# A graph layer on one core: attention's steps laid out by TensorE's load, and seven in place of five pairs of edge tiles fetched by ScalarE's queue

## The reference

```
msg   = relu(x[src] + edge_attr @ w_e + b_e)              # 131072 edges
agg   = segment_sum(msg, dst)                             # src, dst sorted by dst
local = bn1(relu((x + agg) @ w1 + b1) @ w2 + b2 + x)
q,k,v = split(x.reshape(256, 32, 256) @ in_w.T + in_b)    # 256 graphs of 32 nodes
o     = softmax(q k^T / 8) v                              # 4 heads of 64
attn  = bn2(o @ out_w.T + out_b + x)
out   = local + attn
out   = bn3(out + relu(out @ m_w1 + m_b1) @ m_w2 + m_b2)
y     = layernorm(x + out)
```

## Time and profile before

| | |
|---|---|
| median of 3 runs | 1318.26 us (1317.13 to 1326.54) |
| the profiled execution | 1322.04 us, its span 1320.3 us |
| TensorE busy | 1164.2 us, 88% |
| GpSimd busy | 944.2 us, 72% |
| VectorE busy | 824.7 us, 62% |
| ScalarE busy | 543.6 us, 41% |
| mean granted clock of TensorE | 0.96 |

### The profile page before, as it was taken

The page is one execution under the profiler, slowest core; times in us unless marked ns, Lnnn a source line. Parts: engine busy times, 40 slices in busy tenths (PEclk is TensorE's granted clock), DMA queues, the critical chain, the costliest instruction groups (busy, mean ns, idle before and its releaser), DMA issues.

```text
span 1320.3 us, 28247 instructions
## 1 busy us (share of the span) xinstructions
PE 1164.2 (88%) x7309; PEld 650.1 (49%) x7309; DVE 824.7 (62%) x2090; ACT 543.6 (41%) x1077; POOL 944.2 (72%) x1004
## 2 busy tenths in 40 slices
PE   5777899899898989988898999989899898999787
PEld 3444454444444444444444445445454455666466
DVE  4665575848557465775747667584765857555464
ACT  1334344444343444533444443444444344344344
POOL 7466647777777777777677777777777777777771
PEclk6989999999989989999999999999999999999899
DMA  8354445565655556555465556556565555555551
GB/s 318 104 165 129 140 124 153 164 190 163 189 158 154 177 154 181 162 174 167 140 186 167 180 157 187 162 155 188 163 181 161 174 160 172 164 166 173 156 147 54
DMA packets 119282, 216.50 MB, mean 164 GB/s; under 512 B 24784, under 2 KB 69584, under 8 KB 119120
## 3 DMA queue, kind: packets, MB, share of 16 engines
q0 software_dynamic: 47808, 130.61, 34.3%
q1 hardware_dynamic: 67312, 79.47, 19.2%
q10 hardware_dynamic: 4000, 4.61, 1.0%
HBM read 197.82 MB, written 16.78 MB: 163 GB/s over the span
## 4 chain that ended last, share of the span: by engine, by line
PE 49%; DVE 14%; POOL 9%; issue 9%; ACTq 9%; ACT 7%; DMA 3%; DVEq 1%; SPq 0%; POOLq 0%
PE bank L839 27%; PE bank L869 11%; POOL xg L432 9%; PE bank L884 7%; ACTq L465 6%; ACT msg L471 4%; DVE bank L683 4%; ACTq L313 2%; DVE mx L728 2%; PE bank L893 2%; DVE dif L733 2%; PE bank L966 2%; DMA xg<-in_x_dram,srcs 2%; DVE aggT L716 2%; DMA xT<-in_xT_dram 1%
## 5 line engine op out<-in xcount | busy, mean ns | idle before, releaser
L432 POOL DMA_INDIRECT xg<-in_x_dram,srcs x996 | 943.3, 947 | 349.7 <-issue 285.3
L471 ACT ACTIVATE msg<-bank 128x512 f32<-128x512 f32 x512 | 277.9, 594 | 528.9 <-PE bank L869 280.8
L683 DVE TENSOR_TENSOR bank<-xg,bank 128x512 f32<-128x512 f32 x498 | 326.1, 689 | 184.2 <-ACT msg L471 97.2
L869 PE MATMUL bank<-we,ea 64*128 64x256 f32 x2048 | 303.2, 416 | 43.1 <-DVE bank L683 42.7
L869 PEld LDWEIGHTS bank<-we,ea 64*128 64x128 f32 x2048 | 185.1, 193 | 188.3 <-issue 145.0
L716 DVE TENSOR_TENSOR aggT<-bank,aggT 128x64 f32 x512 | 114.8, 224 | 167.5 <-PE bank L893 114.5
L884 PE MATMUL bank<-msg,onehot 128*32 128x256 f32 x2048 | 142.9, 398 | 56.8 <-ACT msg L471 56.8
L839 PE MATMUL bank<-xT,iwT 128*128 128x512 f32 x256 | 129.8, 631 | 17.4 <-ACT kbd L492 7.4
L839 PE MATMUL bank<-o,m 128*128 128x512 f32 (+2 forms) x352 | 125.4, 490 | 6.5 <-DVE o L760 5.0
L884 PEld LDWEIGHTS bank<-msg,onehot 128*32 128x32 f32 x2048 | 54.7, 111 | 142.2 <-ACT msg L471 98.4
L839 PE MATMUL bank<-h,m 128*128 128x512 f32 (+2 forms) x352 | 116.4, 479 | 0.7 <-ACT h L531 0.7
(11 more groups left out here) (92 smaller groups left out, 944.7 us busy)
## 6 DMA issues: line engine op xcount, KB each, us to landing
rows<-in_x_dram SPq DMA_DIRECT2D x2304, 1.0 KB
ea<-in_ea_dram SPq DMA_DIRECT2D x128, 256.0 KB
rows<-in_x_dram ACTq DMA_DIRECT2D x1280, 1.0 KB
xg<-in_x_dram,srcs POOLq DMA_INDIRECT x996
xT<-in_xT_dram SPq DMA_DIRECT2D x32, 256.0 KB, 3.6
aggT<-in_xT_dram SPq DMA_DIRECT2D x32, 256.0 KB
oT_dram<-oT SPq DMA_DIRECT2D x32, 256.0 KB, 3.5
xn<-in_x_dram SPq DMA_DIRECT2D x32, 256.0 KB
```

Of the source, the lines that this page charges most:

```text
L432: pool.indirect_dma_start(xg[:, slot % NX, n * C:(n + 1) * C], None, t["x"], bass.IndirectOffsetOnAxis(k.srcs[:, at:at + 1], 0)).then_inc( ...
L471: nc.scalar.activation(msg[:, q % NM, :], EA[q % 4][:, :], ACT.Relu).then_inc(s_msg, 1)
L683: nc.vector.tensor_tensor(EA[q % 4][:, :].rearrange("p (a c) -> p a c", a=2), pair.rearrange("p (a c) -> p a c", a=2), KB[:, 0:C].unsqueez ...
L869: ins = nc.tensor.matmul(EA[(2 * d + pair) % 4][:, two * C:(two + 1) * C], ea[rows, n % NEA, at:at + P], k.we[rows, :], start=False, stop= ...
```

## The change

Two things. Attention's table of turns is replaced by a plan (`plan_heads`): each step of TensorE has a cost, each stage of a node block too, a turn has room for 52, up to 16 more may be borrowed, and what is over counts against the next turn; in each turn at most one step is placed, once its `xT` and its `oT` buffer are free. `xT` is loaded one turn after the block that frees its buffer. And ScalarE's queue fetches seven pairs, each in 28 turns with nine or ten rows followed by seven without, 35 in all; GpSimd gathers 496 pairs in place of 498.

```
-ACT_ROWS, ACT_CYCLE, ACT_LEAD = 5, 50, 6
+ACT_ROWS, ACT_CYCLE, ACT_LEAD = 7, 35, 6
...
-HEADS = {"q": (0, 2), "k": (3, 5), "sc": (6, 8), "soft": (7, 9), "v": (10, 11), "av": (13, 14)}
-HEADS_EARLY = {"q": (0, 0), "k": (1, 1), "sc": (2, 3), "soft": (3, 4), "v": (4, 4), "av": (5, 6)}
...
+STEPS = [("q", 0, 20), ("q", 1, 20), ("k", 0, 20), ("k", 1, 20), ("sc", 0, 10), ("sc", 1, 10),
+         ("v", 0, 20), ("v", 1, 20), ("av", 0, 10), ("av", 1, 10)]
+NODE_WORK = {"w1": 20, "B": 38, "m1": 20, "m2": 38, "T": 10}
+ROOM, SPARE = 52, 16
...
+    for turn in range(TURNS):
+        load = late + node_work(turn) + (25 if turn % 2 else 18)
+        if J < NJ:
+            stage, _, work = STEPS[step]
+            ready = step or J < NXT or turn >= done[J - NXT] + 4
+            if stage == "av" and J >= NOT:
+                ready = ready and turn > done[J - NOT]
+            if ready and load + work <= ROOM + SPARE:
+                load += work
+                heads[J][stage] = heads[J].get(stage, ()) + (turn,)
+                if stage == "sc":
+                    heads[J]["soft"] = heads[J].get("soft", ()) + (turn + 1,)
...
+        late = max(0.0, load - ROOM)
+    loads = [0, 1, 5, 10] + [done[J - NXT] + 1 for J in range(NXT, NJ)]
...
-                if turn in (1, 7, 13):
-                    load_xT((turn + 5) // 6)
-                if turn % 16 == 10 and NXT <= (turn + 38) // 16 < NJ:
-                    load_xT((turn + 38) // 16)
+                for J in range(1, NJ):
+                    if XT_LOADS[J] == turn:
+                        load_xT(J)
```

More of the change, by code:

```diff
@@ L51 @@
 SP_ROWS, SP_TURNS, SP_LEAD = 9, 242, 9
-ACT_ROWS, ACT_CYCLE, ACT_LEAD = 5, 50, 6
+ACT_ROWS, ACT_CYCLE, ACT_LEAD = 7, 35, 6
 SCALE_TURN, FOLD_TURN, BIAS_TURN = 9, 11, 12
-HEADS = {"q": (0, 2), "k": (3, 5), "sc": (6, 8), "soft": (7, 9), "v": (10, 11), "av": (13, 14)}
-HEADS_EARLY = {"q": (0, 0), "k": (1, 1), "sc": (2, 3), "soft": (3, 4), "v": (4, 4), "av": (5, 6)}
-EARLY = 4
-def heads_base(J):
-    return 7 * J if J < EARLY else 16 * J - 33
 BLOCKS = [(FULL * J, FULL) for J in range(12)] + [
@@ L137, in nodes_in, with node_work, second_layer, plan_heads @@
     return found
-def heads_in(turn, stages):
[L141 to L146, removed]
+STEPS = [("q", 0, 20), ("q", 1, 20), ("k", 0, 20), ("k", 1, 20), ("sc", 0, 10), ("sc", 1, 10),
+         ("v", 0, 20), ("v", 1, 20), ("av", 0, 10), ("av", 1, 10)]
+NODE_WORK = {"w1": 20, "B": 38, "m1": 20, "m2": 38, "T": 10}
+ROOM, SPARE = 52, 16
+def node_work(turn):
+    return sum(NODE_WORK[s] * min(1.0, BLOCKS[b][1] / (128 if s == "m1" else 256))
+               for b, s, _ in nodes_in(turn, tuple(NODE_WORK)))
+def second_layer(b):
+    return max(t for t in range(TURNS) for n, s, _ in nodes_in(t, ("B",)) if n == b)
+def plan_heads():
+    done = [second_layer(covering(FULL * J, FULL * J + FULL)) for J in range(NJ)]
+    heads, J, step, late = [{}], 0, 0, 0.0
+    for turn in range(TURNS):
[10 more added lines that the diff above has]
+                    heads[J]["soft"] = heads[J].get("soft", ()) + (turn + 1,)
+                step += 1
+                if step == len(STEPS):
+                    J, step = J + 1, 0
+                    heads.append({})
+        late = max(0.0, load - ROOM)
+    loads = [0, 1, 5, 10] + [done[J - NXT] + 1 for J in range(NXT, NJ)]
+    return heads[:NJ], loads
+def heads_in(turn, stages):
+    return [(J, s, n) for J in range(NJ) for s in stages
+            for n, at in enumerate(HEADS[J][s]) if at == turn]
 def covering(first, last):
     return max(b for b, (n0, w) in enumerate(BLOCKS) if n0 < last and n0 + w > first)
+HEADS, XT_LOADS = plan_heads()
 def stores_before(unit):
```

## The result

The changed kernel takes 1432.6 us (median of four runs, 1429.19 to 1435.76), the kernel before 1322.0 us beside it: a ratio of 1.084, 95% interval 1.078 to 1.089. The change costs 109 us of span, 1429.3 against 1320.3. The direction was forecast, the size was not: 1358 us and a range up to 1410.

What follows compares the result with a forecast made beforehand. Consumers slower than GpSimd early, ScalarE's rows delaying messages later; GpSimd working almost to the end. Terms 38, 147, 817.5, 91, 185 and 82 made 1361 us of span, 1358 on the median; range 1335 to 1410, chance 0.50.

Steps and rivals of the forecast that it cites:

- The mechanism: ScalarE's queue: rows wait behind activations and messages behind rows; seven pairs add 1.30 us to each turn with rows.
- the price of a pair of turns: Turns with rows: between a floor of 10.0 and 12.5 us fully exposed; mean 10.9, or 5.45 a turn.
- the 2.32 us: Pair of turns, even batch's end to next copy: messages 1.08, sum 1.07 and three hand-overs, part of the floor.
- go to the floor, 10.0: About half the pairs, with nothing late on ScalarE in the even turn, take 10.0 us; the others 11.8.
- a sign of being right: In a stretch with rows, a pair of turns should take 10.5 to 11.3 us.
- 8.85 and 11.0: Kernel before, us per pair: 8.85 with nothing late on ScalarE in the even turn, 11.0 for the others.
- the 0.55 us a turn: Kernel before: a turn with rows costs 4.96 us, one in the rest 4.41; the difference was laid to ScalarE's rows.
- The rests: 42 turns without rows on ScalarE's queue, among those with rows: 4.41 us each, 185 us in all.
- The plan's gain: Early turns: one attention step a turn brings turns 3 to 30 to 147 us, 23 less; turn 3 starts near 38.
- The faster rival: ScalarE's sequencer issues rows while activations still wait for semaphores, so GpSimd alone sets the pace: 1280 us, chance 0.25.
- my own sentence: ScalarE's sequencer does not go past a waiting activation; batches start 0.07 us after the last activation started.
- The worst rival: Turns with rows: everything exposed, TensorE's idle time lowering its clock; 5.85 us a turn, 1423 us, chance 0.08.

Runs made afterwards that it cites:

- plan5: Changed kernel with its new attention plan, but five pairs in 50 turns on ScalarE's queue as before: 1304.8 us, 0.985 of the kernel before.
- rows7: Kernel before, attention's old table kept, with seven pairs in 35 turns on ScalarE's queue: 1483.9 us, 1.120 of the kernel before.
- rows0: Kernel before with no rows on ScalarE's queue, GpSimd making 1006 gathers: 1319.2 us, 0.996 of the kernel before.
- halves7: Changed kernel with a turn's rows in two halves, behind the messages and behind the copy: 1319.2 us, 0.993 of the kernel before.
- halves5: Changed kernel with five pairs in 50 turns, a turn's rows in two halves, behind messages and copy: 1287.9 us, 0.973 of the kernel before.
- plan0: Changed kernel with its new attention plan and no rows on ScalarE's queue, GpSimd making 1006 gathers: 1294.3 us, 0.977 of the kernel before.

## Why the prediction was right in direction and too small

**The mechanism** held: rows on ScalarE's queue, in line with the messages. The page of the chain, the waits and plan5 against rows7 all say so.

**The step that failed** is the price of a pair of turns, and in it one term: the 2.32 us "from the end of the even batch to the next copy". Of the 69 us between the forecast's sum and the measured span, 39 lie in the 150 turns with rows. "About half" of the pairs were to "go to the floor, 10.0", the others to 11.8, with a mean of 10.9 or 5.45 a turn. By the node stage in the even turn, 33 pairs with B or m2 average 10.78 us and 34 with w1, m1 or T average 12.12; the mean of the 67 is 11.46, above the 10.5 to 11.3 that was named as a sign of being right. In the forecast's own terms, read from the trace in us:

| from copy to copy | forecast | measured |
|---|---|---|
| copy to the odd batch | 0.07 | 0.10 |
| both batches | 7.46 | 7.44 |
| between them (0.15 and what stands late) | 1.05 | 1.04 |
| end of the even batch to the next copy | 2.32 | 2.88 |
| sum | 10.90 | 11.46 |

So all 0.56 us that are missing lie in that term: 0.28 x 150 turns = 42 us of the 39 in the table. The 2.32 adds up the messages, the sum and the hand-overs and leaves out what TensorE does between them., which the forecast names for it, give 451.06 - (446.94 + 1.21) = 2.91: TensorE runs an attention step there, and the sum only behind it.

```profile
448.01 1.98 PE L839 MATMUL bank<-xT,iwT 128*128 128x512 f32 x4
```

2.32 is the shortest of the 70 such pairs of the kernel before (their median is 3.07), and I had put this minimum where the mean belonged. In the changed kernel 27 of the 67 pairs run at it and the median is 2.46; the long ones lift the mean. Seven pairs take over 4 us and make up nearly half of the 0.56, and six of these seven hold a second softmax step in their even turn. What a shorter softmax would give back there no run shows.

The starting point was off in the same way. The two kinds of pairs average 9.58 and 10.28 us in the kernel before, not 8.85 and 11.0. And the 0.55 us a turn that the forecast put down to ScalarE's rows was not theirs: rows0, without any, takes 741.6 us for the same 150 turns, 4.94 a turn, against 4.89 before. There GpSimd sets the pace.

**The rests** are the second term, 19 us. I took 4.41 a turn from two stretches of the earlier trace rows, and those were light: the four rests of the kernel before average 4.58. The six of the changed kernel take 4.85 a turn. The same 42 turns took 205.7 us before, with rows in most of them, and 204.5 in halves7, so the absence of rows there saves next to nothing. Which work sets their time no run took apart.

**The plan's gain** was right in kind. Turn 3 starts at 33.7 (38 forecast), turns 3 to 30 take 155.8 (147). With five pairs they take 139.8, so the longer batches ate 16 of the 30 us.

**The faster rival** is out as a mechanism. In 98 odd turns with rows, the first of them starts 0.11 us or more after the end of TensorE's sum, for which the copy ahead of it waits, 0.13 at the median. The page "Perfetto Trace Analysis" of the Trainium skill, section "DVE / Act Engine Instruction", has the sequencer go on once a waiting instruction is pushed into the wait queue. The trace does not agree where the semaphore is still open. But my own sentence, that no row goes past an activation, is too strong as well. In 24 of the 98 the first row starts before the copy does, by up to 1.15 us, since the copy was released and only queued for the engine:

```profile
859.72 1.38 ACT L523 ACTIVATE kbd<-bank,vecT 64x512 f32<-64x512 f32 x2 [0.30 <-PE bank L870]
860.81 0.23 ACTq L496 DMA_DIRECT2D rows<-in_x_dram  x1
861.12 0.81 ACT L556 ACTIVATE z<-o,c,s 128x512 f32<-128x512 f32 x1
861.14 0.88 ACTq L496 DMA_DIRECT2D rows<-in_x_dram  x3
861.96 0.37 ACT L507 COPY agg<-bank 128x256 f32<-128x256 f32 x1
```

The sum ended at 860.68, and the first row follows at 860.81, past z and the copy.

The rival's time, 1280, is nearly reached by halves5 all the same, by cutting the batch. **The worst rival**, everything exposed at 5.85 a turn, gave 1423 with a chance of 0.08; with 5.72 it was nearest. Its clock changed little: 0.92 to 0.97 of full speed in stretches with rows, 0.94 to 0.99 before, and TensorE's busy time grew by 23.6 us in all. How much of that reached the span no run shows.

## What to carry to other kernels

Work that only a sequencer does, such as issuing small DMAs and loading addresses, is not in an engine's busy share. Here it was paid for by the length of the piece in which it stood ahead of something others wait for, and by what stood behind it. Cut such work into pieces that fit the gaps that are there anyway before deciding how much of it there may be. And price a line of dependent work with the mean of its parts over many turns; its quickest instance is a floor only.

## What was not expected of the hardware

ScalarE's sequencer passes activations that are released and wait for their turn on the engine, but not one whose semaphore is still open: behind a copy that waits for TensorE's sum, the first row came 0.11 us or more after the sum's end in all 98 batches. And the cost of issuing rises steeply, not in proportion: at 2.43 us of it a turn the kernel takes 11 us more than with none at all (plan5, plan0), at 2.98 us 37, at 3.73 us 138, while 3.73 us in two pieces cost 25. These are net of what the rows spare GpSimd: 10, 12 and 14 gathers of 1.25 us, that is 12.5, 15 and 17.5 us.
